# A decoder layer on one core: the raw products of the feed-forward down projection issued for two steps at a time

## The reference, cut to what matters

```
gate = x @ gate_w.T            # 2048 tokens x 2048 inner units
up   = x @ up_w.T
inter = silu(gate) * up
y = inter @ down_w.T           # 2048 tokens x 512 outputs
out = layernorm(x + y)
```

## Time and profile before

| | us |
|---|---|
| three runs | 626.80, 627.12, 628.09 |
| median | 627.12 |
| the profiled execution | 628.18 |
| its span (first to last instruction) | 626.30 |

### The profile page before, as it was taken

How to read it: one execution, slowest core, us unless ns; L and a number is a source line. 1 busy time by engine, 2 the same in 40 slices (tenths; PEclk the granted TensorE clock), 3 DMA queues, 4 the chain that set the end, 5 groups by cost and what they waited for, 6 DMA issues and landing times.

```text
span 626.3 us, 12076 instructions
## 1 busy us (share of the span) xinstructions
PE 601.2 (96%) x4292; PEld 474.3 (76%) x4292; DVE 412.8 (66%) x842; ACT 359.5 (57%) x1026; POOL 286.5 (46%) x344
## 2 busy tenths in 40 slices
PE   8999999999999999999998798899899999999995
PEld 8778887888887978888877586676677677767663
DVE  3365676777677767776767955666586658556644
ACT  5665756666665767666757845544455645544351
POOL 0728189889775777849557551164002100200111
PEclk9999999999999999999999998999999999999999
DMA  9622002615241042102133287544806741684011
GB/s 320 230 69 101 2 2 102 177 53 177 85 136 68 3 146 78 48 32 79 46 116 92 102 212 178 174 102 93 227 17 155 217 100 28 158 218 69 2 67 68
DMA packets 34571, 68.09 MB, mean 109 GB/s; under 512 B 14160, under 2 KB 16336, under 8 KB 33744
## 3 DMA queue, kind: packets, MB, share of 16 engines
q1 hardware_dynamic: 29296, 52.51, 29.4%
q0 software_dynamic: 4928, 14.29, 7.4%
q10 hardware_dynamic: 288, 0.52, 0.3%
HBM read 42.14 MB, written 13.93 MB: 90 GB/s over the span
## 4 chain that ended last, share of the span: by engine, by line
PE 85%; DVE 5%; ACT 3%; DMA 3%; SPq 1%; issue 1%; POOL 0%; POOLq 0%; ACTq 0%; DVEq 0%
PE bank L464 16%; PE bank L466 14%; PE bank L465 14%; PE bank L651 8%; PE bank L1509 7%; PE bank L639 5%; PE bank L673 5%; PE bank L1484 4%; PE bank L1418 2%; DMA x_in<-x 2%; SPq L1449 1%; ACT probs L840 1%; PE bank L659 1%; PE bank L690 1%; PE bank L563 1%
## 5 line engine op out<-in xcount | busy, mean ns | idle before, releaser
L840 ACT ACTIVATE probs<-bank,minus_max 128x256 f32<-128x256 f32 x256 | 118.6, 487 | 38.9 <-DVE minus_max L1007 38.6
L1007 DVE TENSOR_REDUCE minus_max<-bank 128x2 f32<-128x512 f32 x128 | 79.5, 682 | 46.3 <-PE bank L639 46.3
L1018 DVE COPY probsT<-bank 128x512 f32<-128x512 f32 x96 | 59.8, 677 | 19.7 <-PE bank L651 19.6
L1698 DVE TENSOR_TENSOR hidden<-bank,silu 128x512 f32<-128x512 f32 x64 | 44.0, 687 | 42.5 <-PE bank L466 26.0
L651 PE MATMUL bank<-ident,probs 128*128 128x128 f32 x512 | 62.5, 273 | 3.1 <-ACT probs L840 3.1
L651 PEld LDWEIGHTS bank<-ident,probs 128*128 128x128 f32 x512 | 57.0, 140 | 7.4 <-ACT probs L840 5.0
L1653 ACT CAST hidden_hi_lo<-hidden 128x512 fp32r<-128x512 f32 x64 | 39.8, 621 | 38.6 <-DVE hidden L1698 38.2
L1647 ACT ACTIVATE silu<-bank 128x512 f32<-128x512 f32 x64 | 38.1, 596 | 38.0 <-PE bank L466 37.3
L1702 DVE TENSOR_TENSOR hidden_hi_lo<-hidden,hidden_hi_lo 128x512 fp32r<-128x512 f32 x64 | 44.4, 694 | 23.4 <-ACT hidden_hi_lo L1653 22.6
L1782 POOL TENSOR_TENSOR ffn_var_eps<-ffn_mean_var,constants 128x4 f32<-128x4 f32 x3 | 0.6, 200 | 125.6 <-DVE ffn_mean_var L1732 125.6
L1509 PE MATMUL bank<-hidden_hi_lo,down_raw 64*128 64x512 f32 x384 | 55.8, 409 | 0.7 <-DVE outs_T L1711 0.6
(11 more groups left out here) (201 smaller groups left out, 1594.4 us busy)
## 6 DMA issues: line engine op xcount, KB each, us to landing
features_by_group<-features_by_cell SPq DMA_DIRECT2D x128, 128.0 KB, 2.3
ctx_squared_T<-in_ctxT SPq DMA_DIRECT2D x8, 512.0 KB, 5.8
xres<-in_x SPq DMA_DIRECT2D x8, 512.0 KB, 4.5
x_in<-x SPq DMA_DIRECT2D x16, 256.0 KB, 3.3
makers_out<-makers_rounded SPq DMA_DIRECT2D x9, 416.0 KB, 4.8
xin_T<-in_xT SPq DMA_DIRECT2D x7, 512.0 KB, 4.0
x<-x_rows SPq DMA_DIRECT2D x7, 512.0 KB, 5.0
x_residual<-x POOLq DMA_DIRECT2D x3, 1024.0 KB, 6.9
```

The source lines that it names most:

```text
L840: inc(nc.scalar.activation(probs[:, g, t, :], S[g][:, t * T:(t + 1) * T], ACT.Exp, bias=nmax[:, g, t:t + 1], accum_out=rsum[:, t, g:g + 1] ...
L1007: inc(nc.vector.tensor_reduce(nmax[:, g, :], S[g][:].rearrange("p (t k) -> p t k", t=TT), AX.X, ALU.max, negate=True), "max")
L1018: inc(nc.vector.tensor_copy(probsT[:, g, :, :], S[g][:].rearrange("p (k t) -> p k t", k=2)), "ptv")
L1698: inc(nc.vector.tensor_tensor(hm[:], U[:], sg[:], ALU.mult), "hm")
```

## The change

Raw products are no longer done in every step, but in every even one, for the two steps before: twenty-four matmuls of 64 rows in a row, in half j = 1. `raw_of` gives the steps of a burst: in step 0 of block n the steps 6 and 7 of the block before, in step 2 the steps 0 and 1, and so on; step 7 of the last block does step 6 alone, and the last step's products stand at the end as before. Since the inner units of a step are now read two steps later, they get a third buffer (`hidden_hi_lo_third`, picked by `hid_of`), and `act_hh` waits for the products of five halves earlier, not three.

In an odd step the moments are spread: two matmuls behind each half's gate and up. In an even step all four stay in half 0. `pe_polynomials` of pair 0 moves from (n, 5, 1) to (n, 6, 1), behind the burst of steps 4 and 5. To make room for the third buffer the moments' split copy exists once for both pairs (`moments_hi_lo`), with waits in `act_moments` to match.

The core of the diff:

```diff
@@ -408,9 +408,9 @@
     hid = sb("hidden_hi_lo", [P, 2, 2, JT, BLK], F32R, late)
     yq = sb("outs_T", [P, Q, BLK], F32, late)
     by_poly = sb("down_by_moment", [P, 2, 2, D], F32R, late)
-    mom = sb("moments_hi_lo", [P, 2, 2, BLK], F32R, late)
+    mom = sb("moments_hi_lo", [P, 2, BLK], F32R, late)
     by_segment = [by_segment_0, sb("by_segment1", [P, Q * JT, P], F32R, late)]
-    sb("unused_three", [P, Q * JT, P], F32, late)
+    hid3 = sb("hidden_hi_lo_third", [P, 2, JT, BLK], F32R, late)
     sg = sb("silu", [P, BLK], F32, late)
     res = sb("x2_residual", [P, BT, D], F32, late)
 
...
@@ -1507,11 +1507,11 @@
             for b in range(2):
                 rows_ = slice(b * PART, (b + 1) * PART)
                 last = nc.tensor.matmul(Dn[2 * pair + b][:], raw[st][rows_, lo_w, j * P:(j + 1) * P],
-                                        hid[rows_, st % 2, lo_h, j, :], start=pr == j == k == 0, stop=False)
+                                        hid_of(n, st)[rows_, lo_h, j, :], start=pr == j == k == 0, stop=False)
         if st == MOVED_STEP and j == 0:
             pe.wait_ge(s["hused"], index(n, st, j))
             for lo_w, lo_h in ((0, 0), (0, 1), (1, 0)):
-                last = nc.tensor.matmul(Dn[1][:], raw[STEPS][0:PART, lo_w, 0:P], hid[0:PART, st % 2, lo_h, 0, :],
+                last = nc.tensor.matmul(Dn[1][:], raw[STEPS][0:PART, lo_w, 0:P], hid_of(n, st)[0:PART, lo_h, 0, :],
                                         start=False, stop=False)
         inc(last, "hused")
 
...
@@ -1614,18 +1614,30 @@
                 wait(pe, "ws", i - 1)
             pe_job(pe, i, job_bank(i))
 
+    def raw_of(n, st):
+        if (n, st) == (NB - 1, STEPS - 1):
+            return [(n, st - 1)]
+        if st % 2 or n == st == 0:
+            return []
+        return [(n, st - 2), (n, st - 1)] if st else [(n - 1, STEPS - 2), (n - 1, STEPS - 1)]
+
     def pe_step(pe, n, st):
         for j in range(JT):
             pe_gate_up(pe, n, st, j)
             pe_turn(pe, n, st, j, 0)
             pe_fill(pe, n, st, j)
             prev = (n, st - 1) if st else (n - 1, STEPS - 1)
+            burst = raw_of(n, st)
             for i in range(JT):
-                if prev[0] >= 0:
-                    (pe_raw if j else pe_moments)(pe, *prev, i)
+                if prev[0] >= 0 and i == j if not burst else prev[0] >= 0 and j == 0:
+                    pe_moments(pe, *prev, i)
+            if j == 1:
+                for at in burst:
+                    for i in range(JT):
+                        pe_raw(pe, *at, i)
             if n and st == 0 and j == 1:
                 pe_polynomials(pe, n - 1, 1)
-            if st == 5 and j == 1:
+            if st == 6 and j == 1:
                 pe_polynomials(pe, n, 0)
             if n and (st, j) == (1, 1):
                 pe_outs(pe, n - 1, 0)
@@ -1646,16 +1658,20 @@
         wait(act, "hm", i)
         inc(nc.scalar.activation(sg[:], G[:], ACT.Silu), "silu")
 
+    def hid_of(n, st):
+        slot = (STEPS * n + st) % 3
+        return hid3[:] if slot == 2 else hid[:, slot, :, :, :]
+
     def act_hh(act, n, st, j):
         i = index(n, st, j)
         act.wait_ge(s["hm"], i + 1)
-        wait(act, "hused", i - 3)
-        inc(nc.scalar.copy(hid[:, st % 2, 0, j, :], hm[:]), "hh")
+        wait(act, "hused", i - 5)
+        inc(nc.scalar.copy(hid_of(n, st)[:, 0, j, :], hm[:]), "hh")
 
     def act_moments(act, n, pair):
         act.wait_ge(s["mo"], 2 * n + pair + 1)
-        wait(act, "db" if pair else "kap", 2 * n if pair else Q * n)
-        inc(nc.scalar.copy(mom[:, pair, 0, :], Mo[:]), "moh")
+        wait(act, "kap" if pair else "db", Q * n + Q if pair else 2 * n)
+        inc(nc.scalar.copy(mom[:, 0, :], Mo[:]), "moh")
 
     def act_outs(act, n, q):
         wait(act, "db" if q >= 2 else "da", 2 * n + q % 2 + 1)
@@ -1699,11 +1715,11 @@
 
     def dve_hl(dve, n, st, j):
         dve.wait_ge(s["hh"], index(n, st, j) + 1)
-        inc(nc.vector.tensor_tensor(hid[:, st % 2, 1, j, :], hm[:], hid[:, st % 2, 0, j, :].bitcast(F32), ALU.subtract), "hl")
+        inc(nc.vector.tensor_tensor(hid_of(n, st)[:, 1, j, :], hm[:], hid_of(n, st)[:, 0, j, :].bitcast(F32), ALU.subtract), "hl")
 
     def dve_moments(dve, n, pair):
         dve.wait_ge(s["moh"], 2 * n + pair + 1)
-        inc(nc.vector.tensor_tensor(mom[:, pair, 1, :], Mo[:], mom[:, pair, 0, :].bitcast(F32), ALU.subtract), "mol")
+        inc(nc.vector.tensor_tensor(mom[:, 1, :], Mo[:], mom[:, 0, :].bitcast(F32), ALU.subtract), "mol")
 
     def dve_outs(dve, n, q):
         wait(dve, "db" if q >= 2 else "da", 2 * n + q % 2 + 1)
```

More of the change, by code:

```diff
@@ L1483, in pe_moments @@
         for h in range(2):
-            last = nc.tensor.matmul(Mo[:], by_segment[pair][:, JT * pr + j, :], hid[:, st % 2, h, j, :],
+            last = nc.tensor.matmul(Mo[:], by_segment[pair][:, JT * pr + j, :], hid_of(n, st)[:, h, j, :],
                                     start=pr == h == j == 0, stop=pr == Q - 1 and h == j == 1)
@@ L1523, in pe_polynomials @@
         for q in (2 - own, 3 - own):
-            last = three(Dn[q][:], [by_poly[:, pair, h, q * P:(q + 1) * P] for h in range(2)], [mom[:, pair, h, :] for h in range(2)],
+            last = three(Dn[q][:], [by_poly[:, pair, h, q * P:(q + 1) * P] for h in range(2)], [mom[:, h, :] for h in range(2)],
                          False, pair == 1)
@@ L1530, in pe_polynomials @@
                 q, rows_ = own + b, slice((1 - b) * PART, (2 - b) * PART)
-                last = nc.tensor.matmul(Dn[q][:], by_poly[rows_, pair, lo_w, q * P:(q + 1) * P], mom[rows_, pair, lo_m, :],
+                last = nc.tensor.matmul(Dn[q][:], by_poly[rows_, pair, lo_w, q * P:(q + 1) * P], mom[rows_, lo_m, :],
                                         start=False, stop=pair == 1 and k == 2)
```

## The result

The changed kernel takes 650.16 us (median of four runs, 649.92 to 650.57) against 627.61 us before: the ratio is 1.0354, with a 95% interval of 1.0336 to 1.0372. The change makes the kernel 22.5 us slower. The forecast was 645.3 us with a range of 637.5 to 651.5.

A forecast was written before the change was run, and what follows sets the result against it. TensorE, busy 96% of the span, was taken to bound the kernel. Terms summed to +14.9 us, +18.2 with the clock's 3.3; 628.18 + 18.2 = 646.4 profiled, less 1.06 gives 645.3 us, range 637.5 to 651.5.

The forecast's parts named there:

- The bursts: Bursts of raw products fall from 32 to 17; fifteen fewer at 0.38 us for entering and leaving: -5.7 us.
- The stops in front of (n, 6, 0): In blocks 1 to 3 TensorE's gate product waits for ACT's silu of (n, 5, 1): 3.65 us each, 11.0.
- The moments behind the stop: In (n, 6, 0) the moments of (n, 5, 1) wait for the low part: 0.3 us each, 1.0.
- The turns of (n, 7, 0): In blocks 0 to 2 the second feature turn waits for DVE's copy of the first: 0.47 us more each, 1.4.
- The transposes: In (n, 1, 1) they wait for DVE's copies of the quarters: 0.8 us in block 2, 0.7 in block 3, 1.5.
- The chain of one half: Product, high and low part take 2.10 us a half, TensorE 1.86 in odd steps: waits of 2.5 us.
- Block 0: Two stops end with a transfer: 0.75 us of two bursts given back, raw products (1.4) come after them: 2.1.
- The clock: Low clock behind the three new stops in front of (n, 6, 0): 1.1 us each, 3.3, bounds 0 and 6.
- Rival 1: The stops come, the clock stays high: 642.0 us, chance 0.24.
- Rival 3: Faster: statistics done before TensorE needs the silu of (n, 5, 1), stops hidden, only bursts count: 621.4 us, chance 0.05.
- Rival 4: The second step's twelve products pay the burst's entry again, so the 5.7 is not there: 651.0 us, chance 0.04.
- Rival 2: Heavier: half clock at its upper bound, 2.7 us more, and more late halves, 2.5 more: 650.5 us, chance 0.10.

The follow-up runs named there:

- the split kernel: The kernel before with each burst of twelve raw products split into six and six, 28 bursts more: 636.13 us, ratio 1.0128.
- the merge alone: The kernel before with the raw products of steps 6 and 7 in one burst in (n, 0, 1), feature turns as before: 627.32 us, ratio 0.9999.
- single bursts: The kernel with the filler back, with bursts of twelve in steps 0 to 5 of block 0: 629.59 us, ratio 1.0039.
- the stop filled: The changed kernel with fifteen full matmuls, results unread, in each stop behind (n, 5, 1), n = 1, 2, 3: 644.65 us, ratio 1.0274.
- the turns moved: The kernel before with feature turns 8 and 9 in (n, 6, 1) and (n, 7, 0), not both in (n, 7, 0): 626.64 us, ratio 0.9988.
- the filler back: The changed kernel with step 4's raw products and pair 0's polynomials back in (n, 5, 1), step 5 alone in (n, 7, 1): 633.15 us, ratio 1.0072.
- buffers only: The changed kernel's third buffer, later wait and shared moments' buffer, with TensorE's order as in the kernel before: 627.49 us, ratio 0.9995.

## Why the prediction was right

The mechanism held in its main steps. The sizes were less good: most terms that were off were too small, two were too large, and the time came out 4.9 us above the forecast, near the upper end of the range.

- *The bursts, -5.7.* Confirmed: 0.39 us each in block 2 of the split kernel, 8.0 us for 28 in all, with the transfers' stops taking up a part.
- *The stops in front of (n, 6, 0), 11.0.* Three gaps, from the start of the second of the two moment matmuls to the gate product 4.24, 4.23 and 4.36 us; without the slot of 0.23 that is 4.05 each, 12.1. The cut of 0.45 for DVE's backlog was right in kind (DVE starts the product 0.04 after the up product ends, 479.47 against 479.04 + 0.39), but from there to the statistics DVE took 2.29 us (479.47 to 481.76), not the 1.97 of the earlier trace rows, since between them it now waits 0.39 for ACT's copy of the feature turn (480.56).
- *The moments behind the stop, 1.0.* This came to nothing: at the low clock TensorE reached the four moments of (1, 6, 0) only at 488.75, and DVE had the low part ready at 487.44 + 0.69 = 488.13.
- *The turns of (n, 7, 0), 1.4 in all.* The three waits grew from 0.50 to 0.94 each, 1.3; the merge alone, which lengthens only these, shows 1.4. The row of the table rose by 1.8 in all, since a turn of block 0 waits longer too.
- *The transposes, 1.5.* 1.9 in the table, in blocks 2 and 3 as said. *The chain of one half, 2.5.* 1.4 in the row for `hidden`, 1.2 of it in one stop, the one at (0, 6, 0) that was foreseen. The prediction did not have the 1.6 us in the rows for `x2T_hi_lo`, the turns of block 0 that now follow each other closely.
- *Block 0, 2.1.* This term was mis-sized. It gave back two bursts and counted the step's products as late; it did not see that the stop itself, now 3.58 us, would be followed by the low clock: from its gate product to that of (0, 2, 1) 5.83 us pass, 3.38 before, 2.4 more. With single bursts block 0 gives back about 3 us.
- *Restarts, 1.1.* The second matmul does come 0.34 behind the first (485.20 to 485.54 with the stop filled), but no run shows the sum by itself.
- *The clock, 3.3.* Mis-sized too: 4.4 us in blocks 1 to 3 by the filled stop, and the 2.4 in block 0. Rival 1 is out: the low clock came at all three stops, in block 1 with a stretch twice as long as in blocks 2 and 3. The Trainium skill's warning of idle gaps between bursts (TensorE: Matmul & The Clock Gate, "Why this matters for your kernels") is borne out by these runs; the filled stop shows its price with the stop's length held fixed (4.47 and 4.46 us in block 1).

The sum of 18.2 against 22.5 measured is short by 1.1 at the stops, 1.1 at the clock in blocks 1 to 3, 2.4 at the clock in block 0, 1.6 at its turns and 0.4 at the transposes, and long by 1.0 at the moments behind the stop and 1.1 at the chain of one half. Together that is 4.5, against the 4.3 that are missing; that the errors partly cancelled was luck. Rival 3 (faster) fell by the chain of statistics, which takes 6.5 us from the product's start at 479.47 to the silu's end at 485.98. Rival 4 fell by the timeline: in (1, 4, 1) a burst of 24 starts at 474.84 and the next gate product at 477.78, 2.94 us, where twelve pairs alone are 2.80. Rival 2 named the right total (650.5) for a part of the reason only: the clock was heavier, the chain was not.

What stays open is why the low stretch in block 1 was the longer one, and why one transfer lands later in some of the kernels with the turns moved.

## What to carry to other kernels

Before work is moved away from a place, ask which waits of other engines it hides there: in a list that runs in order, an unrelated instruction ahead of the one you need (here a layer-norm output ahead of a silu) is harmless only as long as the filler lasts. A saving per instruction, even one measured right, is gained only where nothing is waited for behind it; of the two merges that were tried by themselves, the one of steps 6 and 7 gained nothing while a stop stood beside it and 3.7 us once that stop was gone (most of them at a late transfer), and the one of steps 2 and 3 gained nothing clear. An idle gap of TensorE of some 4 us costs more than its length, 1.5 us more here.

## What the runs showed of the hardware that was not expected

Matmuls whose result nobody reads, put into a stop that was there anyway, made the kernel 5.5 us faster (650.16 to 644.65) by keeping the clock at 1.00. The length of a stop alone did not say whether the low clock follows. The one at 377.6 to 378 us was 2.17 to 2.21 us long in all twelve traces; the granted clock fell to 0.50 behind it in nine and stayed at 1.00 in three, at 2.19 us in both cases. Elsewhere it fell behind a stop of 1.79 us (434.07, with the filler back) and did not behind one of 2.15 (449.81, buffers only). And a low clock is free where a transfer ends the next stop, as in block 0 here: it only shortens that stop. So a stop's length in a single trace can mislead: the one at (0, 2, 0) is 0.53 and 2.06 us long in two kernels whose TensorE does the same, and the two take the same time.
